# Transposes in two row tiles with a bank each, and a reordered opening, in a two-layer decoder on one core

## The reference

```python
x = _layernorm(x + _L0_attn_ref(x, W_qkv, q_scale, k_scale, W_out))    # 16 heads of 8, causal, Q and K normed
x = _layernorm(x + _L0_xattn_ref(x, ctx, ctx, Wq, bq, ...))            # 16 heads of 8 over 154 context rows
x = _layernorm(x + _L0_ffn_ref(x, gate_w, gate_b, expert_w, expert_b)) # 8 experts, gates >= 0.1 kept
x = _layernorm(x + _L1_attn_ref(x, Wq, bq, ...))                       # linear attention in chunks of 128
x = _layernorm(x + _L1_xattn_ref(x, ctx, Wq, Wkv, Wproj, b_proj))      # 8 heads of 128 over 154 context rows
x = _layernorm(x + _L1_ffn_ref(x, w_gate, w_up, w_down))               # 384 hidden, silu(gate) * up
```

## Time and profile before

| | us |
|---|---|
| runs | 494.35, 491.85, 494.6 (median 494.35) |
| the profiled execution's own time | 493.74 |
| its span | 491.9 |
| TensorE busy in the span | 458.1 (93%) |
| VectorE busy | 384.5 (78%) |
| ScalarE busy | 351.2 (71%) |
| GpSimd busy | 190.2 (39%) |

### The profile page before, as it was taken

One profiled execution on the slowest core, in us unless ns is written; L12 is line 12 of the kernel. 1 busy time (PEld: TensorE's weight loads), 2 busy tenths in 40 slices (PEclk: granted clock), 3 DMA queues, 4 the chain that ended last, 5 costly groups with the idle time before them and its releaser, 6 DMA issues.

```text
span 491.9 us, 12390 instructions
## 1 busy us (share of the span) xinstructions
PE 458.1 (93%) x4416; PEld 307.2 (62%) x4416; DVE 384.5 (78%) x1133; ACT 351.2 (71%) x893; POOL 190.2 (39%) x365
## 2 busy tenths in 40 slices
PE   5567989998999999999999999999999999999994
PEld 2344557655546546666778555658754756996894
DVE  3559998799899999997788888858788678554465
ACT  3326676866858769887776688986767878969743
POOL 8760001570101644344143232334414537646352
PEclk9689999999999999999999999999999999999999
DMA  7650310032300213001110000030000000000001
GB/s 240 152 148 4 105 31 25 4 86 73 88 4 23 66 39 85 17 2 26 35 35 21 6 3 2 4 88 4 2 13 13 0 2 1 1 2 1 1 1 43
DMA packets 27185, 18.40 MB, mean 37 GB/s; under 512 B 8217, under 2 KB 26773, under 8 KB 26997
## 3 DMA queue, kind: packets, MB, share of 16 engines
q1 hardware_dynamic: 23413, 15.44, 11.8%
q10 hardware_dynamic: 3712, 2.17, 1.7%
HBM read 5.58 MB, written 1.05 MB: 13 GB/s over the span
## 4 chain that ended last, share of the span: by engine, by line
PE 74%; DVE 9%; POOL 6%; issue 3%; ACT 3%; DMA 2%; SPq 2%; ACTq 0%; POOLq 0%; DVEq 0%
PE psum L1051 11%; PE psum L1372 6%; PE psum L1162 6%; PE psum L1395 6%; PE psum L1308 6%; PE psum L1103 5%; PE psum L1130 4%; DVE nmax L1788 4%; PE psum L1406 4%; PE psum L1152 3%; PE psum L1149 3%; PE psum L1417 2%; PE psum L1190 2%; PE psum L1082 2%; PE psum L1109 1%
## 5 line engine op out<-in xcount | busy, mean ns | idle before, releaser
L1537 ACT ACTIVATE EX<-psum 128x1024 f32<-128x1024 f32 (+1 forms) x128 | 118.5, 976 | 8.7 <-PE psum L1136 4.3
L1788 DVE TENSOR_REDUCE nmax<-psum 128x2 f32<-128x768 f32 (+1 forms) x96 | 77.5, 861 | 7.4 <-PE psum L1109 7.2
L1783 DVE TENSOR_REDUCE nmax<-psum 128x4 f32<-128x616 f32 (+1 forms) x80 | 68.1, 876 | 2.9 <-PE psum L1103 2.6
L1103 PE MATMUL psum<-K,Q 64*128 64x154 bf16 (+4 forms) x512 | 50.9, 268 | 5.9 <-issue 4.5
L1014 POOL TENSOR_TENSOR GP<-REST,xrs 128x512 f32<-128x512 f32 (+1 forms) x48 | 32.5, 700 | 41.4 <-DVE xrs L2025 27.6
L1130 PE MATMUL psum<-Q,K 64*128 64x512 bf16 (+3 forms) x320 | 44.7, 315 | 1.6 <-DVE nmax L1788 1.2
L1620 ACT ACTIVATE REST<-psum,nxmax 128x154 f32<-128x154 f32 x96 | 36.2, 395 | 10.7 <-DVE nxmax L2015 9.8
L1444 ACT COPY pvraw<-psum 128x512 f32<-128x512 f32 x32 | 18.7, 585 | 34.3 <-PE psum L1162 24.6
L1103 PEld LDWEIGHTS psum<-K,Q 64*128 64x128 bf16 x512 | 21.4, 95 | 28.2 <-issue 19.1
L1162 PE MATMUL psum<-EX,V 128*32 128x256 f32 (+3 forms) x512 | 37.8, 435 | 0.1
L945 POOL TENSOR_SCALAR rstd_rest<-moments_rest 128x2 f32<-128x2 f32 x32 | 7.3, 228 | 79.1 <-DVE moments_rest L1831 78.7
(11 more groups left out here) (338 smaller groups left out, 1162.4 us busy)
## 6 DMA issues: line engine op xcount, KB each, us to landing
Q<-xparts SPq DMA_DIRECT2D x24, 128.0 KB
Q<-parts SPq DMA_DIRECT2D x21, 128.0 KB
K<-parts SPq DMA_DIRECT2D x21, 128.0 KB
X<-in_x SPq DMA_DIRECT2D x4, 256.0 KB, 3.6
Q<-in_L_xattn_Wkv SPq DMA_DIRECT2D x1, 1024.0 KB, 6.6
K<-xkparts SPq DMA_DIRECT2D x24, 38.5 KB
out<-XB_rest SPq DMA_DIRECT2D x6, 128.0 KB, 1.9
Q<-in_L_xattn_Wq SPq DMA_DIRECT2D x1, 512.0 KB, 4.4
```

What stands on the lines that cost most here:

```text
L1103: last = mm(to[:, r, at:at + n], Q6[a][p, b % 2, 2 * g + jj, P * q:P * q + P], K6[a][p, b % 2, 2 * g + jj, 0:n], start=True, stop=bool(a))
L1537: drains(nc.scalar.activation(dst, src, ACT.Exp), key)
L1783: last = vec.tensor_reduce(nmax[:, :, :, q], src[:, :, 0:2 * n].rearrange("p r (j k) -> p r j k", j=2), AX.X, ALU.max, negate=True)
L1788: last = vec.tensor_reduce(nmax[:, :, jj, q], src[:, :, at:at + P * (q + 1)], AX.X, ALU.max, negate=True)
```

## The change

- `cT` and `PT` become steps of two banks. Each of their four transposes of 128 x 128 becomes two of 64 rows x 128 columns, one in each row tile, with a 64-column piece of the identity moving, each into its own bank. The copy of `PT` and the division of `cT` read both banks; the division's one multiply becomes two of half the size.
- `MERGE` and `BANK_OF` are written anew; `in_pair` holds 64 more steps.
- Opening: the clears of `K6[1]` move from ahead of V's copy into `late_zeros`, which now runs behind V's second copy and waits until VectorE has written part 2 of Q and K. For batch 0 part 1 is copied by ScalarE instead of VectorE, and K's remainder has a tile of its own (in `EX`). All of batch 0's placements stand ahead of batch 1's qkv; the last loads of weights from ScalarE's queue stand behind batch 1's qkv copies.
- TensorE gets matmuls of the identity on nothing: six ahead of the first transposes, two ahead of the first qkv.
- For the last batch element the rest's norms are applied by VectorE (subtract mean, times root), without GpSimd's shift.

```diff
-        return [(b, "x0T", 0)]
+        return [(b, "x0T", 0)] + ([(0, "place", 1, 1)] if b == 1 else [])
...
+SPLIT_T = ('cT', 'PT')
...
-    return step[1] in ("S", "ST") and not (step[1] == "ST" and step[2] and step[4] == 2)
+    return step[1] in SPLIT_T or step[1] in ("S", "ST") and not (step[1] == "ST" and step[2] and step[4] == 2)
...
+        def first_left(w):
+            return EX[:, 0, :] if w else left[:, :]
...
+        def by_tile(key, blocks_):
+            return pair(key)[:, :, 0:TILE * blocks_].rearrange("p r (n t) -> p n r t", t=TILE)
...
-            step(nc.gpsimd.memset(words(K6[1].rearrange("p b h t -> p (b h) t")), 0.0))
-            step(nc.gpsimd.memset(K6[1].rearrange("p b h t -> p (b h) t").bitcast(F32)[
-                :, :, 0:C // 2], TWO_ONES))
             def late_zeros():
-                pool.wait_ge(qk_normed, 1)
+                pool.wait_ge(part_ready[0][2], 2)
+                step(nc.gpsimd.memset(words(K6[1].rearrange("p b h t -> p (b h) t")), 0.0))
+                step(nc.gpsimd.memset(K6[1].rearrange("p b h t -> p (b h) t").bitcast(F32)[
+                    :, :, 0:C // 2], TWO_ONES))
...
-                    late_zeros()
                     return
...
+                if b == 0 and y:
+                    late_zeros()
...
-                step(root(of.rstd, of.moments, LN_EPS))
-                shifted(of.shift, of.moments, of.rstd, 2).then_inc(rest_rstd_ready[z], 1)
+                last = root(of.rstd, of.moments, LN_EPS)
+                if b < B - 1:
+                    step(last)
+                    last = shifted(of.shift, of.moments, of.rstd, 2)
+                last.then_inc(rest_rstd_ready[z], 1)
...
+            def keep_busy(to, count):
+                for _ in range(count):
+                    mm(to[:, 0:P], ident[:, :], ident[:, :], start=True, stop=True)
...
                 to = fill(key)
+                if in_pair(key):
+                    for at, src in pieces:
+                        for r in R:
+                            p = slice(TILE * r, TILE * r + TILE)
+                            last = nc.tensor.transpose(
+                                pair(key)[:, r, at // 2:at // 2 + TILE], src[p], ident[p, p])
+                    fills_(last, key)
+                    return
...
+                    if b == 0:
+                        keep_busy(fill((0, "x0T", 0)), 6)
...
+                    if b == 0:
+                        keep_busy(fill(key), 2)
                     drained(pe, (b, "x0T", 0))
...
+                if b == 0 and w:
+                    for v in range(2):
+                        drained(act, (0, "qkT", v))
+                        copy(parts[:, v, 1, :], first_left(v)).then_inc(part_ready[0][1], 1)
...
+                if b == B - 1:
+                    return
                 z, of = slot(b, a), half_of(b, a)
...
-                drains(vec.tensor_tensor(
-                    ctx[a][:, :, 4 * g:4 * g + 4, :], src[:, :, :, 0:HD],
...
+                for r in R:
+                    last = vec.tensor_tensor(
+                        ctx[a][:, :, 4 * g + 2 * r:4 * g + 2 * r + 2, :], src[:, r, :, :, 0:HD],
...
+            def last_norm(b, h, n=None):
+                if n is None or b < B - 1:
+                    return
+                z, of = slot(b, h), half_of(b, h)
+                dve.wait_ge(rest_rstd_ready[z], norms_until(b, n))
+                dst = of.XB if n == 5 else of.X[n + 1]
+                for i in range(2):
+                    last = vec.tensor_scalar(dst[:, i, :], of.Y[:, i, :], of.moments[:, i, 0:1],
+                                             of.rstd[:, i:i + 1], ALU.subtract, ALU.mult)
+                last.then_inc(rest_x_ready[z], 1)
```

More of the change, by code:

```diff
@@ L354 @@
[L354 to L359, removed]
+    "024613570246124602324256740156240626420634062406420642043602426402645206420462046206"
@@ L360 @@
+    "406125064230164302461302674152630142601465712340671245036714250673142056731405627310"
+    "462756102475612045716204571260547230647320416732451067324510673245160324516032467014"
+    "3620745260174230645273016452713"
 )
@@ L1076, in qkv @@
             def qkv(b, n):
+                key = (b, "qkv", n)
                 if n == 0:
+                    if b == 0:
+                        keep_busy(fill(key), 2)
                     drained(pe, (b, "x0T", 0))
@@ L1485, in qkv @@
                 drains(copy(qkn[:, n, :, :].rearrange("p w d -> p (w d)"), src[:, 0:3 * D]), key)
+                if b == 1 and n == NB - 1:
+                    load(late)
             def k_norm(b):
@@ L1627, in cross_T @@
                 g = u % 2
-                src = filled(act, key).rearrange("p (h q) -> p h q", h=4)
+                filled(act, key)
                 if u >= 2:
                     filled(act, (b, "XO", h, u // 2 - 1))
-                drains(copy(half_of(b, h).XPT[:, 4 * g:4 * g + 4, :], src), key)
+                drains(copy(half_of(b, h).XPT[:, 4 * g:4 * g + 4, :].rearrange(
+                    "p h (r t) -> p h r t", t=TILE), by_tile(key, 4)), key)
             def cross_rest_T(b, h, u):
@@ L1758, in qkT @@
                 left_free()
-                drains(vec.scalar_tensor_tensor(left[:, :], bank(key),
+                rest = first_left(w) if b == 0 else left[:, :]
+                drains(vec.scalar_tensor_tensor(rest, bank(key),
                                                 col("k_scale") if w else col(QS),
                                                 parts[:, w, 0, :], ALU.mult, ALU.subtract), key)
-                drained(dve, key)
-                split(left[:, :], parts[:, w, :, :], part_ready[0], 2 * b + w + 1)
+                if b:
+                    drained(dve, key)
+                    split(rest, parts[:, w, :, :], part_ready[0], 2 * b + w + 1)
+                elif w:
+                    for v in range(2):
+                        dve.wait_ge(part_ready[0][1], v + 1)
+                        vec.tensor_tensor(parts[:, v, 2, :], first_left(v), parts[:, v, 1, :],
+                                          ALU.subtract).then_inc(part_ready[0][2], 1)
+                    splits.append((part_ready[0][2], 2))
             def cross_split(b, w):
@@ L1815, in divided @@
                     drained(dve, (b0, "cT", a0, g0))
-                src = filled(dve, key).rearrange("p (n h d) -> p n h d", n=NB, h=4)
-                step(vec.reciprocal(rsum[:, :, :], src[:, :, :, HD]))
-                now()
-                drains(vec.tensor_tensor(
-                    ctx[a][:, :, 4 * g:4 * g + 4, :], src[:, :, :, 0:HD],
-                    rsum[:, :, :].rearrange("p n (h o) -> p n h o", o=1).to_broadcast(
-                        [P, NB, 4, HD]), ALU.mult), key)
+                filled(dve, key)
+                src = pair(key)[:, :, 0:TILE * NB].rearrange("p r (n h d) -> p r n h d", h=2, d=32)
+                recip = rsum[:, :, :].rearrange("p (r m) h -> p r (m h)", r=2)
+                step(vec.reciprocal(recip, pair(key)[:, :, 0:TILE * NB].rearrange(
+                    "p r (m d) -> p r m d", d=32)[:, :, :, HD]))
+                now()
+                for r in R:
+                    last = vec.tensor_tensor(
+                        ctx[a][:, :, 4 * g + 2 * r:4 * g + 2 * r + 2, :], src[:, r, :, :, 0:HD],
+                        recip[:, r, :].rearrange("p (n h o) -> p n h o", h=2, o=1).to_broadcast(
+                            [P, NB, 2, HD]), ALU.mult)
+                drains(last, key)
             def moments_of(y, stats_, moments_, blocks, ready):
@@ L2073, in cross_weights @@
                 last.then_inc(x0_weights_ready, 1)
-            work = {"qk_moments": qk_moments, "qk_norm": qk_norm, "qkT": qkT,
+            def last_norm(b, h, n=None):
[8 more added lines that the diff above has]
+                last.then_inc(rest_x_ready[z], 1)
+            work = {"norm": last_norm, "qk_moments": qk_moments, "qk_norm": qk_norm, "qkT": qkT,
                     "xk": lambda b: cross_split(b, 1), "xq": lambda b: cross_split(b, 0),
```

40 lines of the change are left out of this document (21 added, 19 removed).

## The result

| | before | after |
|---|---|---|
| median, us (16 runs each, same chip) | 493.18 | 496.66 |
| ratio, 95% interval | | 1.0056 [1.0033, 1.0078] |
| span of the profiled execution | 491.9 | 493.7 |

What follows compares the result with a forecast made beforehand. No engine bounds up to 36.9 us, VectorE to 61.5, then TensorE to 480. Terms -3.7 + 1.7 + 0.5 - 5.2 - 0.8 - 1.0 = -8.5 from the median 494.35 gave 485.9 us, range 479 to 498.

Steps and rivals of the forecast that it cites:

- rival (4): Whole order: the new order removes waits counted at nothing, up to 4 us more, 482; chance 0.60 together with the forecast.
- Rival (2): 61 to 200 us: two-bank steps wait for both banks, VectorE comes to bound; middle's -3.7 gone, 489.6; chance 0.13.
- the transposes' gain of 3.7: Middle part, about 61 to 400 us: 44 groups save 8.8 us, 33 more mode changes cost 5.1, sum -3.7.
- the opening: Up to the first scores: root 2.1 us earlier, then 3.1 more; -5.2 at the end, between -2 and -6.
- the last norms: Last batch element: shift gone at the end -0.8 us, seven mostly covered norms -1.0, between 0 and -3.
- -3.7 + 1.7 + 0.5: Split transposes: middle part -3.7 us, last part +1.7 as mode changes outweigh savings, VectorE's extra multiplies +0.5.
- the root: Batch 0's opening, root starting at 14.29: 2.1 us earlier, from clears and copy gone (0.8) and the clock (1.3).
- the rest: Opening behind the root: remainders without casts, then ScalarE's six placements, bring the first scores 3.1 us earlier.
- My -1.3 for the clock: First eight qkv matmuls: idle-time matmuls bring the rise to 2.4 GHz earlier, -1.3 us, between 0 and -2.1.
- (1): Half transposes: weight loads of the two row tiles go one after the other, only mode changes left, 498.1; chance 0.15.
- (3): Opening gives only 2 us, since the placements' landing and not their issue ends the wait; 489.1; chance 0.12.
- the signs that I had listed as telling against me: Pairs 0.11 or more apart, TensorE idle time 61 to 400 us up over 3 us, or qkv matmuls 0.66 apart throughout.

Runs made afterwards that it cites:

- new_order_whole: The changed kernel with cT and PT back as whole transposes of one bank each; 499.01 us, ratio 1.0110 to before.
- old_order_norm_moved: Kernel before with changed opening, last norms on VectorE, and the first half's norm 4 moved ahead of the last XO; 490.82 us, ratio 0.9942.
- old_order_opening: The kernel before with the changed opening alone, whole transposes and last norms as before; 490.92 us, ratio 0.9939.
- old_order_opening_cold: old_order_opening without the eight idle-time matmuls of the identity; 491.20 us, ratio 0.9954.
- old_order_few_split: old_order_norm_moved with four cT steps split where a second bank lies empty, four other steps on other banks; 491.58 us, ratio 0.9953.

## Why the prediction was wrong

**The failed step** is the rewritten order, which I priced only by its mode changes; its waits were put at nothing, with "TensorE waits little now", and in rival (4) even below nothing. With the same opening and last norms, new_order_whole lies at 1.0110 and old_order_norm_moved at 0.9942: 1.7%, or 8.3 us, with an interval of some 2 us either way, for the order (sequence and banks together). Rival (2) had the mechanism half right, steps of two banks that cost waits, but I let it take away only the transposes' gain of 3.7, and I looked for it on the wrong side. In the new order a second bank costs nothing that shows; what costs is the order that was written to make room for it.

By measured terms, as shares of before: opening and last norms -0.6%, order +1.7%, second bank 0, half transposes -0.6%. They give the +0.6% of the result, but as steps between neighbouring runs they must, so this is a breakdown and no check. Against my sum, the order was mis-sized by 8.3 us, the opening by 2.2 and the last norms by 1.8, and the transposes gave 1.4 more than I had put. The last norms stand at 0 in this, since in old_order_norm_moved they bring nothing over old_order_opening; without them the new order would cost 12.7 us more.

**The transposes** were right in their parts: pairs 0.06 apart, 0.24 a group (0.30 with the bare load), mode changes 0.095, and 57 more of them between 36 and 480 us of the trace where the orders gave 65 in all. Net I had -3.7 + 1.7 + 0.5 = -1.5 and the runs show -2.9, the same within their interval. In the Trainium skill, "TensorEngine Tiling (Array Packing)", Key Properties, the drain between tiling modes is stated; the trace bears it out with 0.093 to 0.103 us.

**The opening** met the first scores to 0.03 us, in part by luck: the root came 2.8 us earlier where I had put 2.1, and the rest brought 2.4 where I had put 3.1. Its worth at the end was wrong: 3.0 instead of 5.2. What I had left out is that the lead first runs into a longer wait for the first `mT` (2.17 to 2.20 us where it was 1.36), behind which 1.2 to 1.7 of it are gone, and that the clock falls at another place in each execution; in the trace without such a fall nearly 5 us reach the end. My -1.3 for the clock was too small for the eight qkv matmuls, which are 2.1 us shorter; 1.1 of that came without the matmuls on nothing too (4.36 us in the trace of old_order_opening_cold), and what those are worth at the end, 0.3 us, isn't told from nothing.

**The last norms** were wrong in the old order, since I named nothing that stands ahead of them in VectorE's queue. That is the very question which a moved step has to be asked. In the new order they bring 12.7 us; the trace shows one chain of root, shift and ScalarE that TensorE waits for, and the clock falls behind it, but the 12.7 us were not taken apart further.

**Rivals.** (1) is false: pairs take 0.06. (3) is false in its reason, since the first scores came when forecast; its 2 us for the opening are 1.0 from the 3.0 measured, my 5.2 are 2.2 from them. (4) has the wrong sign. Of the signs that I had listed as telling against me, one came: TensorE's idle time between 61 and 400 us grew by 4.2 us by the stages, over the 3 that I had set.

**What stays open.** Whether the 8.3 us come from the sequence alone or also from its banks is argued, not shown. Which stretch of the new sequence makes scores and exponentials wait for each other was not isolated; the placements are the only local cause shown, worth 1.4 to 1.8 us, not clear of noise. Whether another order with room for the second bank could keep the waits of before was not tried.

## What to carry to other kernels

When an edit needs a second bank for many steps, its price is the order of work that makes room for it, and that price does not stand in the rows of the edited instructions. Where the rewritten order can be had, time it with the old instructions before believing the gain: here that run alone (499.0 against 490.8) would have told. A step moved to another engine is priced by what stands ahead of it in that engine's queue. A lead won in the opening is priced at the end and over several executions, since the next wait takes a part of it and the clock may fall at another place in each.

## What the runs showed of the hardware

- Float32 transposes in two row tiles run side by side: pairs of 64 x 64 start 0.060 to 0.066 us apart, where whole transposes are 0.11 apart, and behind a mode change a group takes 0.06 more. A change between row tiles, column tiles and the whole array costs 0.093 to 0.103.
- A wait of TensorE can be paid twice: the clock sometimes falls behind it. In the change 1.6 us of waiting were followed by 3.41 us at a granted clock of 0.50, in the run without last norms 3.4 us by 3.65 at 0.53. TensorE was busy when the clock fell in old_order_opening (1.26 us of 1.26 up to 38.16), 1.3 us behind a wait of 2.20. It does not always fall: behind the same step's wait of 2.17 in old_order_few_split it stayed at 1.00, and so it did behind waits of 1.58, 1.51 and 1.45 at 62 us in three other traces of the new order.
- A single placement in SP's queue can take 2.16 us to issue (57.11) where its neighbours take 0.54 to 0.61. Eight of the change's placements take over 1 us, and none does in the trace of before (0.82 at most); what makes them slow was not isolated.
